# First stage of a two-layer decoder kernel: a new layout for the split queries and keys, with part of it copied by VectorE

## The reference, cut to what matters

```
Q = (X @ Wq.T + bq) ; K = (X @ Wk.T + bk) ; V = (X @ Wv.T + bv)      # 16 heads of 16
scores = einsum('bqhd,bkhd->bhqk', Q, K), masked causally, softmax over k
out = einsum('bhqk,bkhd->bqhd', attn, V) @ Wo.T + bo ; x = layernorm(x + out)
```

## Time and profile before

| | |
|---|---|
| median of 3 runs | 1100.72 us (1100.09 to 1102.75) |
| profiled execution, time | 1104.31 us |
| profiled execution, span from first to last instruction | 1102.2 us |
| TensorE busy (matmul), weight load | 985.8 us (89%), 732.8 us (66%) |
| VectorE, ScalarE, GpSimd busy | 887.2 us (80%), 638.6 us (58%), 533.6 us (48%) |
| mean granted TensorE clock | 0.956 of full |
| stacking transfers (L831) | 96 of 128 KB, median 5.6 us from issue to landing |

### The profile page before, as it was taken

How to read it: one execution, slowest core, us unless ns; L and a number is a source line. 1 busy time by engine, 2 the same in 40 slices (tenths; PEclk the granted TensorE clock), 3 DMA queues, 4 the chain that set the end, 5 groups by cost and what they waited for, 6 DMA issues and landing times. The chain is left out here.

```text
span 1102.2 us, 25412 instructions
## 1 busy us (share of the span) xinstructions
PE 985.8 (89%) x8610; PEld 732.8 (66%) x8610; DVE 887.2 (80%) x2031; ACT 638.6 (58%) x1626; POOL 533.6 (48%) x983
## 2 busy tenths in 40 slices
PE   3769899977989858999999999999996999979996
PEld 3556666655656427888888888888874666546664
DVE  1359899967979857999999999999765899668885
ACT  2325556536979814555555555555553999845453
POOL 6337778865645533344444444444333465533322
PEclk8879999989999959999999999999997999989999
DMA  7989998865696400000000000004002566311111
GB/s 135 167 170 156 205 177 142 142 128 127 157 217 166 134 25 10 16 23 28 25 23 23 23 23 23 28 18 113 13 18 57 147 167 164 101 34 50 53 58 34
DMA packets 113631, 97.04 MB, mean 88 GB/s; under 512 B 16688, under 2 KB 106080, under 8 KB 113504
## 3 DMA queue, kind: packets, MB, share of 16 engines
q1 hardware_dynamic: 100032, 84.28, 35.1%
q10 hardware_dynamic: 11504, 8.98, 3.0%
q0 software_dynamic: 1968, 2.16, 1.2%
HBM read 64.97 MB, written 19.99 MB: 77 GB/s over the span
## 5 line engine op out<-in xcount | busy, mean ns | idle before, releaser
L431 DVE TENSOR_REDUCE ca_nm<-p_p 128x2 f32<-128x512 f32 x256 | 163.2, 677 | 17.3 <-PE p_p L321 16.1
L576 ACT ACTIVATE ca_pt<-p_p 128x512 f32<-128x512 f32 x256 | 142.8, 598 | 13.4 <-PE p_p L340 8.2
L1980 ACT ACTIVATE la_pq<-p_p,la_nm 128x128 f32<-128x128 f32 x256 | 90.3, 366 | 37.2 <-DVE la_nm L2083 37.2
L340 PE MATMUL p_p<-ca_qs,ca_ks 128*128 128x256 bf16 x512 | 100.9, 280 | 5.8 <-ACT ca_qs L568 2.4
L321 PE MATMUL p_p<-ca_ks,ca_qs 96*128 96x256 bf16 x512 | 99.3, 278 | 4.0 <-DVE ca_nm L431 2.1
L72 POOL TENSOR_TENSOR ca_pt<-la_lt,one 64x1024 f32<-64x1024 f32 x32 | 60.4, 1889 | 61.4 <-ACT la_lt L1959 60.2
L568 ACT ACTIVATE ca_qs<-p_p 32x1024 bf16<-32x1024 bf16 x64 | 65.1, 1017 | 24.7 <-PE p_p L330 23.3
L1964 ACT ACTIVATE la_qq<-p_p 128x512 f32<-128x512 f32 x32 | 19.1, 597 | 99.1 <-PE p_p L1796 99.1
L1827 PE MATMUL p_p<-ca_pt,la_qq 128*128 128x128 f32 x512 | 70.5, 281 | 0.3 <-POOL ca_pt L72 0.3
L356 PE MATMUL p_p<-ca_pt,ca_va 128*32 128x256 f32 x1024 | 70.4, 393 | 0.0
L1111 DVE TENSOR_REDUCE sa_nm<-p_p 128x4 f32<-128x512 f32 x64 | 43.8, 685 | 29.4 <-PE p_p L968 28.7
(11 more groups left out here) (265 smaller groups left out, 2757.3 us busy)
## 6 DMA issues: line engine op xcount, KB each, us to landing
sa_qks<-sa_qkp SPq DMA_DIRECT2D x96, 128.0 KB, 5.6
ca_qs<-q_parts SPq DMA_DIRECT2D x32, 192.0 KB, 3.2
ca_ks<-k_parts SPq DMA_DIRECT2D x32, 192.0 KB, 3.6
ca_qs<-q_parts SPq DMA_DIRECT2D x32, 128.0 KB, 3.2
ca_ks<-k_parts SPq DMA_DIRECT2D x32, 128.0 KB, 3.6
ca_ct<-in_ctx_t SPq DMA_DIRECT2D x32, 128.0 KB, 3.6
ca_xr<-x_state SPq DMA_DIRECT2D x32, 128.0 KB, 2.1
x_state<-ca_xn SPq DMA_DIRECT2D x32, 128.0 KB, 2.0
```

The costliest lines, as they stand in the source:

```text
L340: last = pe.matmul(p_e[n % 2][:, kc, :], KS[b % 4][:, h, 128 * kc:128 * kc + 128], QS[b % 4][:, h, :], start=True, stop=True)
L431: dve.tensor_reduce(NM[b % 2][:, h, :], p_s[n % 3][:, :, :], AX.X, ALU.max, negate=True).then_inc(max_done, 1)
L576: act.activation(PT[g][:, j, :, :], p_e[n % 2][:, :, :], ACT.Exp, scale=SCALE).then_inc(exp_done, 1)
L1980: last = act.activation(PQ[g % 2][:, j, :], p_s[g % 2][:, j, :], ACT.Exp, bias=NM[b % 2][:, 4 * g + j:4 * g + j + 1], accum_out=SM[g % 2][ ...
```

## The change

`QKP` becomes [128, 6, 2, 256]: six slots, each with a query part beside a key part. The slots are numbered so that those with the same partner are near each other. ScalarE writes high beside high (slot HIGH) and middle beside middle (slot MIDDLE), each in one instruction as before, and GpSimd writes the low query and low key into their slots in one. The other halves are copies: VectorE's `pair_high(f)` puts the high query into two slots and the high key into two, in two instructions of 128x512; `pair_middle(f)` puts the middle query and the middle key into one slot each, in two of 128x256. Both come at g = 0 of step b for f = b + 2, behind `normalise` and ahead of the chunk's L1480. A stacking transfer then reads 1 KB at a time. The three middle transfers also wait for `mid_paired`. Three small tiles move into one, and `plain` into a buffer used later.

```diff
+LOW_QUERY, LOW_KEY, MIDDLE_KEY, MIDDLE_QUERY, HIGH, MIDDLE = range(6)
...
-        plain = [sb(f"plain{n}", [128, 128], BF16) for n in range(2)]
-        BQK = [sb(f"b{n}", [128, KC], F32) for n in range(2)]
+        small = sb("small", [128, 16], F32)
+        BQK = [small[:, KC * n:KC * n + KC] for n in range(2)]
...
-        QKP = [sb(f"qkp{u}", [128, 2, 3, D], BF16) for u in range(2)]
+        QKP = [sb(f"qkp{u}", [128, NT, 2, D], BF16) for u in range(2)]
...
+        plain = [PT[1][:, n, :].bitcast(BF16)[:, 0:128] for n in range(2)]
...
-                both = QKP[f % 2][:, :, :, :].rearrange("p n t c -> p (n t) c")
-                for t in range(NT):
-                    q, k = Q_TERMS[t], 3 + K_TERMS[t]
-                    if max(q, k - 3) == lowest:
-                        sp.dma_start(QKS[f % 3][HD * t:HD * t + HD, :, :, :], both[:, q:k + 1:k - q, :]).then_inc(stack_loaded[f % 3], 16)
+                for t in ((HIGH,), (MIDDLE, MIDDLE_KEY, MIDDLE_QUERY), (LOW_KEY, LOW_QUERY))[lowest]:
+                    sp.dma_start(QKS[f % 3][HD * t:HD * t + HD, :, :, :], QKP[f % 2][:, t, :, :]).then_inc(stack_loaded[f % 3], 16)
...
                 sp.wait_ge(qk_mid, f + 1)
+                sp.wait_ge(mid_paired, 2 * f + 2)
                 place(f, 1)
...
+            def pair_high(f):
+
+                dve.wait_ge(qk_hi, f + 1)
+                pairs = QKP[f % 2]
+                dve.tensor_copy(pairs[:, LOW_KEY:MIDDLE_KEY + 1, 0, :],
+                                pairs[:, HIGH:HIGH + 1, 0, :].to_broadcast([128, 2, D])).then_inc(hi_paired, 1)
+                dve.tensor_copy(pairs[:, LOW_QUERY:MIDDLE_QUERY + 1:MIDDLE_QUERY, 1, :],
+                                pairs[:, HIGH:HIGH + 1, 1, :].to_broadcast([128, 2, D])).then_inc(hi_paired, 1)
+
+            def pair_middle(f):
+
+                dve.wait_ge(qk_mid, f + 1)
+                dve.wait_ge(hi_paired, 2 * f + 2)
+                pairs = QKP[f % 2]
+                dve.tensor_copy(pairs[:, MIDDLE_QUERY, 0, :], pairs[:, MIDDLE, 0, :]).then_inc(mid_paired, 1)
+                dve.tensor_copy(pairs[:, MIDDLE_KEY, 1, :], pairs[:, MIDDLE, 1, :]).then_inc(mid_paired, 1)
...
                 bias_values(f)
+                pair_high(f)
                 context_low(f)
+                pair_middle(f)
...
+                    if g == 0 and values_of(b):
+                        pair_high(b + 2)
+                        pair_middle(b + 2)
...
             def query_key_low(f):
                 pool.wait_ge(qk_mid, f + 1)
-                pool.tensor_tensor(QKP[f % 2][:, :, 2, :], QKR[:, :, :], QKP[f % 2][:, :, 1, :], ALU.subtract).then_inc(qk_lo, 1)
+                if f >= 2:
+                    pool.wait_ge(stack_loaded[(f - 2) % 3], STACK_LOADS * ((f - 2) // 3 + 1))
+                low = QKP[f % 2][:, LOW_QUERY:LOW_KEY + 1, :, :].rearrange("p t n c -> p (t n) c")[:, 0:4:3, :]
+                pool.tensor_tensor(low, QKR[:, :, :], QKP[f % 2][:, MIDDLE, :, :], ALU.subtract).then_inc(qk_lo, 1)
...
-                act.activation(QKP[f % 2][:, :, 0, :], QK[:, :, :], ACT.Copy).then_inc(qk_hi, 1)
+                act.activation(QKP[f % 2][:, HIGH, :, :], QK[:, :, :], ACT.Copy).then_inc(qk_hi, 1)
...
-                act.activation(QKP[f % 2][:, :, 1, :], QKR[:, :, :], ACT.Copy).then_inc(qk_mid, 1)
+                act.activation(QKP[f % 2][:, MIDDLE, :, :], QKR[:, :, :], ACT.Copy).then_inc(qk_mid, 1)
```

More of the change, by code:

```diff
@@ L703, in self_attention @@
         QKR = sb("qkr", [128, 2, D], F32)
-        QKP = [sb(f"qkp{u}", [128, 2, 3, D], BF16) for u in range(2)]
+        QKP = [sb(f"qkp{u}", [128, NT, 2, D], BF16) for u in range(2)]
         CXR = sb("cxr", [128, D], F32)
         CXP = [sb(f"cxp{u}", [128, 3, D], BF16) for u in range(2)]
-        ALN = sb("aln", [128, 2], F32)
+        ALN = small[:, 4:6]
         WO = sb("wo", [128, KC, D], F32)
@@ L726, in self_attention @@
         Y = sb("y", [S, D], F32)
-        ST6 = sb("stats", [S, 6], F32)
-        MV = sb("mv", [S, 2], F32)
-        RS = sb("rstd", [S, 2], F32)
+        ST6, MV, RS = small[:, 6:12], small[:, 12:14], small[:, 14:16]
         XN = [sb(f"xn{u}", [S, D], F32) for u in range(2)]
@@ L756, in self_attention @@
         qk_hi, qk_rest, qk_mid, qk_lo = sem("qk_hi"), sem("qk_rest"), sem("qk_mid"), sem("qk_lo")
+        hi_paired, mid_paired = sem("hi_paired"), sem("mid_paired")
         c_hi, c_rest, c_mid, c_lo = sem("c_hi"), sem("c_rest"), sem("c_mid"), sem("c_lo")
@@ L1190, in query_key_rest @@
                 wait(pool, qk_lo, f)
-                pool.tensor_tensor(QKR[:, :, :], QK[:, :, :], QKP[f % 2][:, :, 0, :], ALU.subtract).then_inc(qk_rest, 1)
+                pool.tensor_tensor(QKR[:, :, :], QK[:, :, :], QKP[f % 2][:, HIGH, :, :], ALU.subtract).then_inc(qk_rest, 1)
             def query_key_low(f):
                 pool.wait_ge(qk_mid, f + 1)
-                pool.tensor_tensor(QKP[f % 2][:, :, 2, :], QKR[:, :, :], QKP[f % 2][:, :, 1, :], ALU.subtract).then_inc(qk_lo, 1)
+                if f >= 2:
+                    pool.wait_ge(stack_loaded[(f - 2) % 3], STACK_LOADS * ((f - 2) // 3 + 1))
+                low = QKP[f % 2][:, LOW_QUERY:LOW_KEY + 1, :, :].rearrange("p t n c -> p (t n) c")[:, 0:4:3, :]
+                pool.tensor_tensor(low, QKR[:, :, :], QKP[f % 2][:, MIDDLE, :, :], ALU.subtract).then_inc(qk_lo, 1)
             def scale(t):
```

## The result

The changed kernel takes 1124.57 us (median of 4 runs, 1120.92 to 1125.31) against 1100.4 us (1097.12 to 1102.75): ratio 1.0206, 95% interval 1.0177 to 1.0235. It is slower by some 24 us, where 16.4 were forecast. The profiled execution took 1124.49 us with a span of 1122.7, 20.5 more than before.

A forecast was written before the change was run, and what follows sets the result against it. TensorE, VectorE and the DMA engines were taken as near full in the ten steps. Ten steps +14.4, b = 2 +1, b = 13 +1 and start 0 make +16.4 on 1100.7: 1117 us, range 1101 to 1131.

The forecast's parts named there:

- A: Rival, as summed: one middle copy held in a step, steps of 14.4 to 15.2 us, 1113 to 1121 us; chance 0.47.
- rival C: Both middle copies held, or TensorE's waits grow to some 3 us and its clock dips: 1122 to 1135 us; chance 0.12.
- ahead of the ten steps: Start of the first stage and b = 2: the start sums to 0, work behind the late middle part costs +1.
- the ten steps: First stage, b = 3 to 12, also quantizing weight chunks: 133.6 us becomes 148, +14.4 us (bounds +3.4 and +25.4).
- behind them: Step b = 13, without a chunk, costs +1 (0 to +2); later stages begin later by the whole amount.
- The transfers: Stacking transfers in SyncE's queue: runs of 1 KB instead of 512 bytes give nearly nothing; rate stays near 100 GB/s.
- The wait: VectorE's pair_middle waits for ScalarE's middle part of the same f, some 0.1 to 1 us in each step.
- The chain: One step from bn_aggr to bn_aggr: copies 5.3, to divide 2.6, to residual add 5.7, back 1.2, sum 14.8 us.
- The hold-ups: GpSimd's low part holds the second middle copy to 5.3 us after bn_aggr; neither held 13.7, both 15.9 us a step.
- D: Rival, faster: transfers pay by run, not byte, so stacks take 4 us instead of 8; 1093 to 1097 us; chance 0.14.
- E: Rival, no change: gain from faster transfers against loss from the copies, 1097.4 to 1104 us; chance 0.09.
- B: Rival: GpSimd and VectorE slip past each other, steps of 13.7 to 14.3 us, 1105 to 1112 us; chance 0.18.

The follow-up runs named there:

- experiment 1: The changed kernel without VectorE's copies and the wait on them, 1 KB transfer runs kept: 1104.34 us, ratio 1.0016 to the kernel before.
- 10: The changed kernel without any copies, with quantize steps 0 to 2 moved behind divide: 1095.15 us, ratio 0.9933 to the kernel before.
- experiment 7: The changed kernel with quantize steps 0 to 2 behind divide and pair_high moved earlier, behind residual at g = 3: 1105.3 us, ratio 1.004.
- 12: The changed kernel with twelve extra TensorE products that nobody reads ahead of the turn of the heads: 1116.73 us, ratio 1.0119.
- experiment 5: The kernel before with quantize steps 0 to 2 moved behind divide and bias_values at g = 1: 1096.61 us, ratio 0.9945.
- experiment 2: The kernel before with the four VectorE copies added, into a spare tile nobody reads, 512-byte transfer runs: 1124.42 us, ratio 1.0218.
- 3: The changed kernel with pair_middle copying the high part, so it needn't wait for ScalarE's middle part: 1117.51 us, ratio 1.0141.
- 4: The changed kernel with pair_middle moved one group later, behind bias_values at g = 1: 1119.48 us, ratio 1.0177.
- experiment 11: The changed kernel with five extra TensorE products that nobody reads ahead of the turn of the heads: 1120.69 us, ratio 1.0148.
- 6: The changed kernel with quantize steps 0 to 2 moved behind divide, copies left in place: 1105.89 us, ratio 1.0027 to the kernel before.

## Why the prediction was right or wrong

The direction and the mechanism were right, and the time came out 7.6 us above the forecast: inside the range, above A's 1113 to 1121 and at the foot of rival C's. By parts of the profile the change cost 5.25 us ahead of the ten steps (+1 forecast), 19.2 in them (+14.4) and -3.9 behind them (+1): 20.5 and not 16.4.

**Right.**

- *The transfers*: worth nothing (experiments 1 and 10), though the DMA engines do work 23 us less; nobody waited. Their rate, mostly 94 to 129 GB/s in experiment 1, is near the 100 that was named, and XT(2)'s wait didn't fall (9.06 us, 7.86 before). The 109 that the prediction worked out for one transfer is near the mean of a window in which only stacks and one load flow (114 in experiment 1), but no ceiling: slices of the earlier trace rows reach 148.
- *The copies*: 0.28 and 0.23 us unheld, against 0.29 and 0.23.
- *The wait*: VectorE waits for ScalarE's line in six of ten steps, 3.6 us in all.
- *The chain*, piece by piece, in a step at full clock: 5.16, 2.45, 5.69 and 1.17 us against 5.3, 2.6, 5.7 and 1.2, 14.47 against 14.8.
- *The hold-ups*: one middle copy of two is held in nine of the ten steps (L1111 median 0.227 us, L1112 1.182), as in A, both in the longest. The Trainium skill ("SBUF — State Buffer", two separate sides) gives the first of the two in time the ports; the trace agrees: in the step shown the first copy starts 0.04 us before GpSimd's low part and isn't held, in the longest it starts 0.02 us after it (155.80 and 155.78 us) and is. But near the border the profile's starts don't decide alone: in experiment 7 normalise starts 0.02 to 0.03 us before GpSimd's remainder in eight steps (166.50 and 166.53 us in one), and takes 1.3 us all the same. That the sum came out in nine steps and its upper bound in one hangs on some 0.04 us, which is luck.
- *TensorE's wait* for the divided rows: 22.1 us, "over 15".
- *No step of 12.4 us* is left; *stacks* hidden, 1.6 us of waits against 1.8.

**Mis-sized: the ten steps, +19.2 where +14.4 stood.** Were all ten at 14.47 us, the sum would be 144.7, +11.1, less than forecast, and the sign "14.8 us apart throughout" failed: five steps last 14.4 to 14.5 us and five 15.9 to 16.6. The other 8 us have three sources.

- *The clock, four steps of 1.4 us.* From divide to the residual add they take 7.07 to 7.09 us instead of 5.69, nearly all of it in the sixteen products of queries and keys, which take 3.25 to 3.6 us instead of 2.05. The prediction took this 5.7 us as fixed ("nothing shortens it") and didn't ask what lengthens it. It had the clock only as part of rival C and took it as a case apart, where it goes with the sum itself: the sum puts a wait of 2 to 3 us for TensorE into each step, and with such waits filled (12) no step had its products slow. One of the ten steps of the kernel before has it too (3.24 us, behind a wait of 1.71), so the change adds three.
- *Late `middle`, 1.55 us.* In the third step the middle copies wait for ScalarE, which has been issuing weight transfers, and divide ends 9.16 us behind bn_aggr. The prediction took `middle` at 3.75 in all ten and charged ScalarE's delays for b = 2 alone.
- *Both middle copies held, 0.8 us.* In the longest step, from 151.95 to 168.58 us, they take 1.22 and 1.08 us and end at 6.07, +0.9, and divide ends at 8.37.

The result is A's chain with less than half of C's condition.

**Mis-sized: ahead of the ten steps, +1 where +5.25 was measured.** The first of the ten starts at 93.69 us and not at 88.44. XT(2) (wait 9.06 against 7.86) and mx_gate's chunk (6.32 against 5.86) came later, where a gain was hoped for; in b = 2 VectorE stands 10.21 us before the middle copy:

```profile
26.52 3.79 PE L917 MATMUL p_p<-sa_xt,sa_w 128*128 128x128 f32 x16 [9.06 <-DMA sa_xt<-in_x_t]
...
80.60 0.23 DVE L1111 COPY sa_qkp<-sa_qkp 128x256 bf16<-128x256 bf16 x1 [10.21 <-ACT sa_qkp L1325]
```

The prediction had +1 (0 to +3) for the work that this wait pushes behind it. But these waits and the start of the ten steps move from profile to profile without the change. XT(2)'s wait is 9.12 us in experiment 5, which has the old layout and no copies, and 7.96 in experiment 2, which has them. XR's first load of the ten is at 86.7 us in experiment 1, 88.6 in 2, 91.4 in 3, 87.0 in 4, 93.2 in the changed kernel, 87.6 before, and at 86.7 in experiment 11, which is the changed kernel but for five products a step. Only the kernels with the order of experiment 5 are apart, at 80.6 to 84.7. With one profile of each kernel, how much of the 5.25 belongs to the change stays open.

**Mis-sized: behind them, +1 where the changed kernel gains.** It is 24.4 us behind at the last stacks and 20.8 at the load of la_wr (393.5 against 372.7 us). The step b = 13, for which +1 stood, takes 11.18 us from bn_aggr to bn_aggr and not 13.00, the next 12.81 and not 15.03. Why wasn't traced. "Later stages begin later by the whole amount" is right from there on: 20.5 us in the span.

**The rivals.** D and E fall by experiments 1 and 10. B's step of 13.7 to 14.3 us is what experiments 3 and 6 come to in their short steps, without the wait and by another order: 14.27 and 13.91; the change itself never gets there (14.41 at the least). C is true in part: the waits have a mean of 2.2 us, and the clock's dips cost some 5.6 us in the ten steps.

**Open.** Why the products are slow in one step and not in the next. TensorE's waits before them are 3.40, 2.00, 2.52 and 2.97 us in the four slow ones and up to 2.74 and 2.95 in the others, so the length of this wait alone doesn't decide. What else does wasn't tried.

## What to carry to other kernels

Price an instruction that is added to an in-order queue by what stands behind it and who waits for that: here 2.9 us of copies and hold-ups in front of divide cost TensorE's wait, then in some steps its clock, and the same copies on ScalarE cost a sixth of it (0.34% against 2.06%). If the new instruction waits for another engine, look at that engine's worst step and not at a typical one. Before making a transfer faster, look whether anyone waits for it. And look first at the order that is there: moving three quantize steps behind the instruction that TensorE waits for, with no copy and no new layout, was worth 0.55% and beats both kernels (with the new layout and the copies on ScalarE it was 0.67%, which the intervals don't tell from 0.55).

## What the runs showed of the hardware that wasn't expected

- A hold-up by GpSimd moves. Take it from one VectorE instruction (L1112, 1.18 to 0.22 us for the copy in its place) and the next of its kind gets it (L1508 and L1510: 0.55 and 0.97 us, 0.17 each unheld). Move the held copy to an earlier place (L1101, 0.86 to 0.26 us in the mean) and normalise behind it gets it (0.64 to 1.16).
- Waits of 1.3 to 3.4 us in nine of ten steps of 14.4 to 16.6 go with slow products in four of them: sixteen take 3.25 to 3.6 us instead of 2.05, and the granted clock of such a step has a mean of 0.89. With the wait filled by products none of ten steps had them slow.
- Inside SBUF, to 16 partitions, runs of 1 KB instead of 512 bytes for the stacks take 13% off the engines' time for the whole queue (65.2% against 75.4% of 225 us, for the same 26.4 MB, of which the stacks are about half) and 0.8 of 5.6 us off the time to landing. That is more than nothing, and much less than half.
